# Seven of eight expert products as block products of a pair of token tiles, in a graph network with a mixture of experts

## The chip, the cores and the metric

One core of one Trainium2 chip runs the whole kernel in one launch. The metric is the device time in microseconds of that core: the median of several runs. A profiled execution gives a span, from its first to its last instruction, which is a little shorter.

## What is computed

`x` is 1250 x 512, there are 40,000 edges (`src`, `dst`), and 8 experts with a 512 x 512 weight each. All arithmetic is float32 in the reference.

```python
h = relu(layernorm(x) @ W1 + b1) @ W2 + b2          # 512 -> 256 -> 512
x = x + h + segment_sum(h[dst], src)                # row src collects h of dst
t = layernorm(x)
gate = softmax(t @ W_gate + b_gate); thr = 0.25 * sigmoid(t @ W_thr + b_thr)
w = relu(gate - thr); w = w / where(sum(w) == 0, 1, sum(w))
x = x + sum over e of w[:, e] * (t @ W_exp[e] + b_exp[e])
```

Every token goes through all 8 experts. The experts are most of the arithmetic.

## The kernel before, in words

The 1250 tokens are 10 tiles of 125 (`TILES`, `R`). Each engine has its own program, written out by hand, and the programs meet in semaphores.

**Head.** TensorE counts edges into an adjacency matrix: VectorE makes one-hot rows by comparison (L639), TensorE multiplies them (L908, float16, 250 columns, 50 windows), ScalarE copies the counts out (L431) and a DMA turns them into `a_t`. Between them stands the first linear layer (L856), and the aggregation (L870, float32) adds the tiles up in five PSUM banks. When the last window is counted, TensorE has 20 matmuls of aggregation left, then the degrees (L933), which need VectorE's sum of all `a_t` (L664, the last one waits for a DMA). VectorE copies the degrees (L685) and adds degree times `b2` to each of the ten tiles (L691). ScalarE copies the aggregate out (L480), and TensorE begins the second linear layer (L946, four tiles at once).

**Second normalization.** For each tile, VectorE adds the layer's output (L699), takes statistics (L705, L712), ScalarE the root (L484) and the normalized tile (L490), TensorE transposes it (L956, four blocks), ScalarE rounds the transposed tile to float16 as `xhi` (L495), VectorE takes the rest as `xlo` (L715), and TensorE multiplies both with the gate's weights (L965, L968). TensorE's order is: transposes of tile i, second layer of tile i + 4, gate of tile i - 1, and, from i = 6 on, a tile of expert 0. VectorE then works out the gate's weights for all tiles in a chain of small operations (L730 to L757), while TensorE goes on with expert 0 in seven banks.

**Experts.** A product in float32 quality is three float16 matmuls: high tokens with high weights, high with low, low with high (L990, L991, L992), summed in PSUM. A tile of an expert is 4 blocks of 128 inputs x 3 = 12 matmuls of 512 columns. Tokens are the stationary operand, loaded before each matmul. VectorE reads each finished tile once (L766: times the gate weight, added to `x_sb`) and adds the expert's bias (L771: `be_sb` in SBUF, times the gate weight). Four PSUM banks rotate. Experts 1 to 6 are a hardware loop of two experts a turn (`expert_loop`), 0 and 7 stand outside it. The weights of the next expert are fetched by SP into one of two stages (L300, 1 MB), rounded by ScalarE (L502: 2048 elements per partition, waiting for the last product that reads the buffer) and completed by VectorE in one operation in the middle of the pass before (L679). GpSimd makes constants in the first 8 us and does nothing after. In the last pass each tile leaves by two DMAs, 112 rows from SP (L331) and 13 from ScalarE's queue (L521), after its last addition.

## Time and profile before

| | us |
|---|---|
| three runs | 384.81, 385.31, 385.79; median 385.31 |
| profiled execution, span | 383.1 |
| profiled execution, its own run time | not recorded |
| TensorE busy | 367.2 (96%), 1892 matmuls |
| VectorE busy | 286.9 (75%) |
| ScalarE busy | 105.2 (27%) |
| GpSimd busy | 6.3 (2%) |
| DMA | 23.87 MB, mean 62 GB/s |

A matmul's record is longer than its turn: matmuls are pipelined, so the time that one costs is read from the distance between starts (or from the chain), not from its duration. The same holds in part for VectorE and ScalarE. The engines' names are PE (TensorE), PEld (its weight load), DVE (VectorE), ACT (ScalarE), POOL (GpSimd) and SP (the queue that starts DMAs); L12 is line 12 of the kernel. The number after the arrow at a line's end is idle time and what ended it.

### The profile page before, as it was taken

What the parts mean: (1) busy time and instruction counts of PE and PEld (TensorE: products, weight loads), DVE (VectorE), ACT (ScalarE), POOL (GpSimd) and SP (SyncE); (2) the same over time, 40 slices, a digit from 0 to 9 for tenths busy, and PEclk for the clock granted to TensorE, in tenths of its full rate; (3) what the DMA queues carried; (4) which work ended last, traced back from release to release, by engine and by line L of the source; (5) the groups of instructions that cost most, each with busy time, mean ns of one, the idle gap of its engine ahead of it and who ended that gap; (6) DMA issues with size and microseconds to landing.
All of it is one profiled execution on the core that took longest, in us unless ns stands there. A gap on an engine that the chain in (4) does not pass through costs nothing.

```text
span 383.1 us, 5937 instructions
## 1 busy us (share of the span) xinstructions
PE 367.2 (96%) x1892; PEld 239.3 (62%) x1892; DVE 286.9 (75%) x440; ACT 105.2 (27%) x189; POOL 6.3 (2%) x33
## 2 busy tenths in 40 slices
PE   2999999999999999999999999999999999999996
PEld 2777787656656563567656666666666666666663
DVE  6799987999999849972897756757657657576553
ACT  5843455556776204555010010010100100100000
POOL 6000000000000000000000000000000000000000
PEclk9999999999999999999999999999999999999999
DMA  8970011222222206300030300300302000000223
GB/s 222 202 245 19 16 39 44 77 69 78 76 72 85 84 15 158 133 34 2 1 111 0 109 2 1 109 0 1 108 0 96 14 0 0 0 0 0 81 84 104
DMA packets 16341, 23.87 MB, mean 62 GB/s; under 512 B 2169, under 2 KB 9216, under 8 KB 16193
## 3 DMA queue, kind: packets, MB, share of 16 engines
q1 hardware_dynamic: 15902, 23.05, 20.3%
q10 hardware_dynamic: 416, 0.53, 0.6%
q8 instruction: 12, 0.20, 0.2%
q14 instruction: 11, 0.09, 0.1%
HBM read 14.77 MB, written 2.56 MB: 45 GB/s over the span
## 4 chain that ended last, share of the span: by engine, by line
PE 80%; DVE 12%; issue 3%; DMA 2%; DVEq 2%; POOL 1%; ACT 0%; ACTq 0%; POOLq 0%
PE ps_g L990 17%; PE ps_g L991 17%; PE ps_g L992 17%; PE ps_g L870 10%; PE ps_w L908 9%; DVE split L639 3%; PE ps_g L856 3%; PE ps_g L946 2%; DMA x_sb<-in_x_dram 2%; DVE x_sb L691 2%; DVE stats L604 2%; DVE x_sb L766 1%; PE ps_w L900 1%; DVE x_sb L771 1%; PE ps_a L956 1%
## 5 line engine op out<-in xcount | busy, mean ns | idle before, releaser
L990 PE MATMUL ps_g<-we_hi,split 128*125 128x512 f16 x304 | 115.4, 380 | 0.7 <-DVE x_sb L766 0.7
L991 PE MATMUL ps_g<-we_lo,split 128*125 128x512 f16 x304 | 115.3, 379 | 0.0
L992 PE MATMUL ps_g<-we_hi,split 128*125 128x512 f16 x304 | 115.2, 379 | 0.0
L639 DVE TENSOR_TENSOR split<-places,keys 125x1536 f16<-125x1536 int16 (+2 forms) x125 | 91.1, 793 | 7.0 <-PE ps_w L908 4.2
L766 DVE SCALAR_TENSOR_TENSOR x_sb<-ps_g,weight_s,x_sb 125x512 f32<-125x512 f32 x76 | 56.9, 749 | 52.1 <-PE ps_g L992 52.1
L771 DVE SCALAR_TENSOR_TENSOR x_sb<-late,weight,x_sb 125x512 f32<-125x512 f32 x80 | 59.9, 750 | 9.5 <-DVE x_sb L766 5.5
L990 PEld LDWEIGHTS ps_g<-we_hi,split 128*125 128x125 f16 x304 | 41.5, 137 | 24.9 <-DVE x_sb L766 1.2
L992 PEld LDWEIGHTS ps_g<-we_hi,split 128*125 128x125 f16 x304 | 41.5, 137 | 24.1
L991 PEld LDWEIGHTS ps_g<-we_lo,split 128*125 128x125 f16 x304 | 41.5, 137 | 23.7
L908 PE MATMUL ps_w<-split 125*128 125x250 f16 x402 | 53.7, 270 | 2.5 <-DVE split L639 1.6
L908 PEld LDWEIGHTS ps_w<-split 125*128 125x128 f16 x402 | 36.9, 97 | 21.2 <-issue 9.4
L870 PE MATMUL ps_g<-late,r_sb 125*128 125x512 f32 (+3 forms) x120 | 49.1, 516 | 0.0
L502 ACT ACTIVATE we_hi<-stage 128x2048 f16<-128x2048 f32 x6 | 11.5, 1911 | 135.0 <-PE ps_g L992 120.9
L399 ACT ACTIVATE places<-iota_pos,win_base 125x512 int16<-125x512 int16 x50 | 35.7, 713 | 0.0
L431 ACT ACTIVATE counts<-ps_w 128x250 f32<-128x250 f32 x50 | 19.0, 379 | 32.0 <-PE ps_g L870 27.4
L870 PEld LDWEIGHTS ps_g<-late,r_sb 125*128 125x128 f32 x120 | 19.5, 191 | 7.8 <-issue 7.2
L856 PE MATMUL ps_g<-w_sb,x_t 128*125 128x256 f32 x80 | 19.7, 389 | 0.1
L679 DVE SCALAR_TENSOR_TENSOR we_lo<-stage,we_hi 128x2048 f16<-128x2048 f32 x8 | 18.3, 2285 | 0.0
L664 DVE TENSOR_TENSOR late<-late 125x1250 f32<-125x1250 f32 x9 | 13.1, 1454 | 4.9 <-DMA late<-counts 4.9
L856 PEld LDWEIGHTS ps_g<-w_sb,x_t 128*125 128x125 f32 x80 | 14.2, 187 | 2.1 <-issue 0.3
L946 PE MATMUL ps_g<-w_sb,early 128*125 128x512 f32 x32 | 14.8, 595 | 0.1
L900 PE MATMUL ps_w<-self_lo,self_pos 128*128 128x250 f16 x50 | 13.6, 273 | 0.7 <-ACT counts L431 0.7
(143 smaller groups left out, 220.2 us busy)
## 6 DMA issues: line engine op xcount, KB each, us to landing
stage<-in_L_ffn_W_exp_dram SPq DMA_DIRECT2D x8, 1024.0 KB, 5.2
late<-counts SPq DMA_DIRECT2D x50, 122.1 KB
x_sb<-in_x_dram SPq DMA_DIRECT2D x5, 448.0 KB, 11.3
out_dram<-x_sb SPq DMA_DIRECT2D x10, 224.0 KB
late<-in_L_ffn_b_exp_dram SPq DMA_DIRECT2D x1, 2000.0 KB
w_sb<-in_L_gnn_W_dram SPq DMA_DIRECT2D x2, 512.0 KB, 10.6
out_dram<-x_sb ACTq DMA_DIRECT2D x10, 26.0 KB
b_sb<-in_L_gnn_b_dram SPq DMA_DIRECT2D x1, 250.0 KB
```

What stands on the lines that cost most here:

```text
L399: nc.scalar.activation(places[w % WPT][:, :, 0:SEG], iota_pos[:, :, :], ACT.Identity, bias=win_base[:, w:w + 1], scale=1.0).then_inc(pos_r ...
L431: nc.scalar.activation(counts[q][:, :], ps_w[w % 2][:, 0:LO], ACT.Copy).then_inc(win_out, 1)
L639: nc.vector.tensor_tensor(hot[hot_at(w, p)][:, 0:n, :].rearrange("p c (k x j) -> p (c k) x j", k=SEGS, j=2), places[w % WPT][:, 0:n, :].re ...
L766: nc.vector.scalar_tensor_tensor(out=x_sb[:, i, :], in0=ps_first[FIRST_AT[i]] if first else ps_exp[(TILES * par + i) % RING], scalar=weigh ...
L771: nc.vector.scalar_tensor_tensor(out=x_sb[:, i, :], in0=be_sb[:, ds(e, 1), :], scalar=weight[:, i, ds(e, 1)], in1=x_sb[:, i, :], op0=ALU.m ...
L856: nc.tensor.matmul(r_bank[i % 2], x_t[i % XTS][:, k, :], w1_sb[:, k, :], start=(k == 0), stop=False)
L870: g = nc.tensor.matmul(ps_g[:, a:z], r_sb[:, i, c * 128:(c + 1) * 128], a_t[i % 3][:, a - c * SW:z - c * SW], start=opens, stop=False, ski ...
L908: mm = nc.tensor.matmul(bank[:, 0:LO], hot[hot_at(w, p)][:, c, 0:SEG], hot[hot_at(w, p)][:, c, SEG:SEG + LO], start=False, stop=False, ski ...
L946: y = nc.tensor.matmul(ps_y[i % YS], g_sb[:, c, tokens[i]], w2_sb[:, c, :], start=(c == 0), stop=(c == KC - 1))
L990: nc.tensor.matmul(bank, xhi[:, k, tokens[i]], hi_w, start=(k == 0), stop=False)
L991: nc.tensor.matmul(bank, xhi[:, k, tokens[i]], lo_w, start=False, stop=False)
L992: mm = nc.tensor.matmul(bank, xlo[:, k, tokens[i]], hi_w, start=False, stop=(k == KD - 1))
```

## The change

**Products.** Expert 0 stays as it was. For experts 1 to 7, two neighbouring tiles of tokens, left (A) and right (B), are taken as a 2 x 2 block matrix with two halves of 256 inputs each (a1, a2; b1, b2), the weight as 2 x 2 blocks of 256 x 256 (B11, B12, B21, B22). Strassen's algorithm in Winograd's form gives all four output blocks from seven products instead of eight. Weight sums: T1 = B12 - B11, T3 = B22 - B12, T2 = B22 - T1, T4 = B21 - T2. Token sums: S1 = b1 + b2, S3 = a1 - b1, S2 = S1 - a1, S4 = a2 - S2. Each product is 2 blocks of 128 inputs x 3 = 6 matmuls of 256 columns. Products share half banks: a bank is read (times the gate weight, into `x_sb`) after some products and goes on accumulating others, so intermediate states are added to several places. In a unit (a pair and an expert; there are 35) six reads result, five of 256 columns and one of 512. Two neighbouring units are interleaved. TensorE's stationary operand is 128 columns wide, the last three being the next tile's or zeros.

**Sums and halves.** GpSimd makes the four weight sums of every expert (128 x 512 float32 each) and the four token sums of every pair (2 x 125 each). ScalarE keeps a float32 copy `xt` of the transposed tile besides `xhi`, and rounds weights in three operations and token sums in one per pair. VectorE takes the low halves, weights in seven operations per expert of 512 elements, token sums in one per pair. For expert 1 this is in the head, between the last count and L685.

**Bias.** `be_sb` and the 80 operations of L771 go. The gate weights are split into high and low, transposed (10 transposes), and multiplied with three stacked copies of the bias (high, high, low): one matmul of 512 columns per tile, two in the first unit of experts 3 to 7, and one addition on VectorE each.

**Form.** The hardware loop over experts is gone; all units are written out. SP loads expert 2 before the bias, and waits for `wb_lo_done` for the others. Outputs leave after P3 (left tile) and P4 (right tile) of expert 7.

```diff
+            def block_sums(e):
+                w = stage[e % 2][:, :].rearrange("p (k f) -> p k f", k=KD)
+                b11, b12, b21, b22 = w[:, 0:2, 0:H], w[:, 0:2, H:D], w[:, 2:4, 0:H], w[:, 2:4, H:D]
+                pool.wait_ge(we_in[e % 2], 16 * (e // 2 + 1))
+                if e > 1:
+                    pool.wait_ge(wb_lo_done, BLOCKS * (e - 1))
+                nc.gpsimd.tensor_tensor(t_sum[:, T1 - T1, :, :], b12, b11, ALU.subtract).then_inc(t_added, 1)
...
+            pool.wait_ge(win_out, NW)
+            block_sums(1)
+            pool.wait_ge(r_done, TILES)
...
+            for j in range(PAIRS):
+                token_sums(j)
+            pool.wait_ge(y_done, TILES)
...
+            for e in range(2, EXP):
+                block_sums(e)
...
+            def high_blocks(e):
...
+                if e == 2:
+                    act.wait_ge(exp_done, TILES)
+                if e > 2:
+                    act.wait_ge(product_done, PRODUCT["P4", PAIRS * (e - 2) - 1])
+                nc.scalar.activation(hi[:, B11, :, :], w[:, 0:2, 0:H], ACT.Copy, scale=WSCALE).then_inc(wb_hi_done, 1)
...
+                act.wait_ge(t_added, 4 * e)
+                nc.scalar.activation(hi[:, T1:T4 + 1, :, :], t_sum[:, :, :, :], ACT.Copy, scale=WSCALE).then_inc(wb_hi_done, 1)
+            high_blocks(1)
             act.wait_ge(g_done, TILES)
...
+                nc.scalar.activation(xt[:, :, tokens[i]], turned_x, ACT.Copy).then_inc(xt_ready, 1)
+                nc.scalar.activation(xhi[:, :, tokens[i]], turned_x, ACT.Copy).then_inc(xhi_ready, 1)
...
+            for q in (B11, B21, B22):
+                low_block(1, q)
             column_sum(TILES - 1)
+            for q in (T1, T2, T3, T4):
+                low_block(1, q)
...
             dve.wait_ge(deg_done, 1)
...
+            for u in range(UNITS + 1):
...
+                lows = {1: (B11, B21), 2: (B22, T1), 3: (T2, T3), 4: (T4,)}.get(j, ()) if e < EXP - 1 else ()
+                if u < UNITS:
+                    add_product("P1", u, y, left, 0, H, 0)
...
+                if u >= 1:
+                    add_product("P7", u - 1, y_was, was_right, H, D, 0)
+                if lows:
+                    low_block(e + 1, lows[0])
...
+                if u >= 1:
+                    add_product("P3", u - 1, x_was, was_left, 0, D, 0)
+                if u < UNITS:
+                    add_product("P6", u, y, left, H, D, 0)
...
+                if u >= 1:
+                    add_product("P4", u - 1, y_was, was_right, 0, H, 0)
+                if lows[1:]:
+                    low_block(e + 1, lows[1])
+                if u < UNITS:
+                    add_product("P5", u, x, right, H, D, H)
...
+            def product(u, halves, q, out_cols, opens):
+                par = expert_of(u) % 2
+                for k, (hi_x, lo_x) in enumerate(halves):
+                    nc.tensor.matmul(out_cols, hi_x, wb_hi[par][:, q, k, :], start=(opens and k == 0), stop=False, skip_group_check=True)
+                    nc.tensor.matmul(out_cols, hi_x, wb_lo[par][:, q, k, :], start=False, stop=False, skip_group_check=True)
+                    mm = nc.tensor.matmul(out_cols, lo_x, wb_hi[par][:, q, k, :], start=False, stop=(k == 1), skip_group_check=True)
+                mm.then_inc(product_done, 1)
...
+            for u in range(UNITS + 1):
...
+                if bias:
+                    bias_tile(2 * (e - 3))
...
+                    pe.wait_ge(acc_step, Y_AFTER[u] if u < 4 else READ["P4", u - 4])
+                    product(u, (tile_of(left, 0), tile_of(left, 1)), B11, y, True)
...
+                    pe.wait_ge(acc_step, READ["P6", u - 1])
+                    product(u - 1, (sum_of(j_was, S3, 0), sum_of(j_was, S3, 1)), T3, y_was, False)
...
+                    pe.wait_ge(acc_step, X_AFTER[u] if u < 3 else READ["P3", u - 3])
+                    product(u, (tile_of(left, 2), tile_of(left, 3)), B21, x[:, 0:H], True)
...
+                    pe.wait_ge(acc_step, READ["P5", u - 1])
+                    product(u - 1, (sum_of(j_was, S4, 0), sum_of(j_was, S4, 1)), B22, x_was[:, H:D], False)
...
+                    pe.wait_ge(acc_step, READ["P1", u])
+                    product(u, (sum_of(j, S2, 0), sum_of(j, S2, 1)), T2, y, False)
...
+                    pe.wait_ge(acc_step, READ["P7", u - 1])
+                    product(u - 1, (tile_of(2 * j_was + 1, 2), tile_of(2 * j_was + 1, 3)), T4, y_was, False)
...
+                    product(u, (sum_of(j, S1, 0), sum_of(j, S1, 1)), T1, x[:, H:D], False)
```

In the order of the text the seven products of a unit are P1, P2, P6, P5 of the unit itself and P7, P3, P4 of the one before; TensorE's order in a step is P1, P7, P2, P3, P6, P4, P5.

## Rows read from the trace of the kernel before

**Rows 1.** Page, part 1: busy time of the engines.

```profile
PE 367.2 (96%) x1892; PEld 239.3 (62%) x1892; DVE 286.9 (75%) x440; ACT 105.2 (27%) x189; POOL 6.3 (2%) x33
```

**Rows 2.** Busy time by stretch; the columns are from:to, length, engines, clock, DMA.

```profile
131.00:144.00 13.00, 12.66 (x51) 7.35 (x49) 6.91 (x10) 0.81 (x4) 0.00 (x0) 1.00 0.12 33
...
181.60:197.95 16.35, 15.62 (x74) 9.62 (x72) 14.82 (x31) 1.35 (x4) 0.00 (x0) 1.00 0.06 10
...
197.95:379.46 181.51, 181.51 (x840) 114.62 (x840) 120.32 (x152) 10.78 (x6) 0.00 (x0) 1.00 0.12 41
...
379.46:383.10 3.64, 0.00 (x1) 0.00 (x0) 0.75 (x1) 0.00 (x0) 0.00 (x0) 1.00 0.24 74
```

**Rows 3.** Groups by line in the stretch of experts 1 to 7.

```profile
L766 DVE SCALAR_TENSOR_TENSOR x_sb<-ps_g,weight_s,x_sb 125x512 f32<-125x512 f32 x72 | 53.9, 749 | 52.1 <-PE ps_g L992 52.1
```

**Rows 4.** Timeline at the start of expert 1 and at the end; start, duration, instruction.

```profile
196.84 0.38 PE L992 MATMUL ps_w<-we_hi,split 128*125 128x512 f16 x1
...
197.95 0.43 PE L990 MATMUL ps_g<-we_hi,split 128*125 128x512 f16 x1 [0.73 <-DVE x_sb L766]
...
379.08 0.38 PE L992 MATMUL ps_g<-we_hi,split 128*125 128x512 f16 x1
...
379.57 0.75 DVE L766 SCALAR_TENSOR_TENSOR x_sb<-ps_g,weight_s,x_sb 125x512 f32<-125x512 f32 x1 [1.18 <-PE ps_g L992]
```

**Rows 5.** Timeline, from the last count to the second linear layer.

```profile
131.12 7.86 PE L870 MATMUL ps_g<-late,r_sb 125*128 125x512 f32 x20
...
131.30 2.29 DVE L679 SCALAR_TENSOR_TENSOR we_lo<-stage,we_hi 128x2048 f16<-128x2048 f32 x1
...
132.25 0.38 ACT L431 ACTIVATE counts<-ps_w 128x250 f32<-128x250 f32 x1 [1.13 <-PE ps_g L870]
...
137.01 1.46 DVE L664 TENSOR_TENSOR late<-late 125x1250 f32<-125x1250 f32 x1 [3.43 <-DMA late<-counts]
...
141.31 6.71 DVE L691 SCALAR_TENSOR_TENSOR x_sb<-b_sb,deg,x_sb 125x512 f32<-125x512 f32 x10
...
143.69 2.38 ACT L480 ACTIVATE early<-ps_g 128x250 f32<-128x250 f32 x3 [11.07 <-PE ps_g L870]
```

**Rows 6.** Chain that ended last, one burst of L908; start, us, what.

```profile
58.38 1.07 PE ps_w L908 x10
```

**Rows 7.** Page, part 5: the edge counting's matmul and its weight load.

```profile
L908 PE MATMUL ps_w<-split 125*128 125x250 f16 x402 | 53.7, 270 | 2.5 <-DVE split L639 1.6
...
L908 PEld LDWEIGHTS ps_w<-split 125*128 125x128 f16 x402 | 36.9, 97 | 21.2 <-issue 9.4
```

**Rows 8.** Timeline, one tile of the second normalization.

```profile
159.24 0.63 PE L956 MATMUL ps_w<-ident,xn 125*128 125x125 f32 x4
...
159.90 0.59 ACT L495 ACTIVATE split<-ps_w 128x500 f16<-128x500 f32 x1 [1.14 <-PE ps_w L956]
...
160.39 0.80 ACT L490 ACTIVATE xn<-x_sb,shift,rstd 125x512 f32<-125x512 f32 x1
...
160.53 0.68 DVE L715 TENSOR_TENSOR split<-ps_w,split 128x500 f16<-128x500 f32 x1 [0.39 <-ACT split L495]
...
161.42 0.35 PE L965 MATMUL ps_g<-wg,split 128*125 128x18 f16 x4
...
161.86 0.63 PE L956 MATMUL ps_a<-ident,xn 125*128 125x125 f32 x4
...
162.32 1.88 PE L946 MATMUL ps_g<-w_sb,early 128*125 128x512 f32 x4
```

**Rows 9.** Timeline of VectorE: the gate's first operation and expert 0's first read.

```profile
181.67 0.25 DVE L730 SCALAR_TENSOR_TENSOR lg_b<-ps_g,bg_sb 125x90 f32<-125x90 f32 x1 [2.17 <-PE ps_g L968]
...
186.17 0.75 DVE L766 SCALAR_TENSOR_TENSOR x_sb<-ps_g,weight_s,x_sb 125x512 f32<-125x512 f32 x1
```

**Rows 10.** Groups by line and shape: ScalarE's rounding, GpSimd's largest operation.

```profile
L502 ACT ACTIVATE we_hi<-stage 128x2048 f16<-128x2048 f32 x6 | 11.5, 1911 | 135.0 <-PE ps_g L992 120.9 <-PE ps_w L992 14.1
...
L381 POOL TENSOR_SCALAR_AFFINE_SELECT self_lo<-self_lo 25x475 f16<-25x475 f16 x1 | 0.8, 779 | 0.0
```

More of the change, by code:

```diff
@@ L101, in gnn_moe @@
         win_base = sb("win_base", [EP, NW])
-        places = [sb(f"places{q}", [EP, PART, HOT], I16) for q in range(WPT)]
+        places_all = sb("places", [128, WPT * PART * HOT], I16)
+        places = [places_all[0:EP, q * PART * HOT:(q + 1) * PART * HOT].rearrange("p (c h) -> p c h", c=PART) for q in range(WPT)]
         base_row = sb("base_row", [ROWS, NW])
@@ L473, in _ @@
                     act.wait_ge(we_in[0], 16)
-                    nc.scalar.activation(we_hi[0][:, :], stage[0][:, :], ACT.Copy, scale=WSCALE).then_inc(we_hi_done, 1)
+                    nc.scalar.activation(we_hi, stage[0][:, :], ACT.Copy, scale=WSCALE).then_inc(we_hi_done, 1)
                 if w == 32:
@@ new lines, in _ @@
+            for i in range(TILES + 2):
+                if i >= 2:
+                    turn(i - 2)
+                if 1 <= i <= TILES:
+                    norm(i - 1)
+                if i < TILES:
+                    deviation(i)
+                if i in SUMS_AT:
+                    high_sums(SUMS_AT[i])
+            act.wait_ge(logits_ready, 1)
+            nc.scalar.activation(ex[:, :, :], lg_c[:, :, :], ACT.Exp).then_inc(exps_ready, 1)
+            nc.scalar.activation(te[:, :], lg_a[:, :, EXP], ACT.Exp, scale=-1.0).then_inc(exps_ready, 1)
@@ new lines, in _ @@
+            for j in range(len(SUMS_AT), PAIRS):
+                high_sums(j)
+            act.wait_ge(weight_ready, 1)
+            nc.scalar.activation(w_hi[:, :, :], weight[:, :, :], ACT.Copy).then_inc(w_hi_done, 1)
+            act.wait_ge(w_hi_done, 1)
+            nc.scalar.activation(w_3[:, :, 0:2 * EXP].rearrange("p t (r e) -> p t r e", r=2),
+                                 w_hi[:, :, :].unsqueeze(2).broadcast_to([R, TILES, 2, EXP]), ACT.Copy).then_inc(w_3_ready, 1)
+            high_blocks(2)
@@ new lines, in _, with tile_of, sum_of @@
+            gate(TILES - 1)
+            for i in range(RING, TILES):
+                first_expert(i)
+            def tile_of(i, k):
+                at = k * N + i * R
+                return split[:, at:at + 128], split[:, KD * N + at:KD * N + at + 128]
+            def sum_of(j, c, k):
+                return s_hi[:, j, c, k, :], s_lo[:, j, c, k, :]
+            def product(u, halves, q, out_cols, opens):
[5 more added lines that the diff above has]
+                mm.then_inc(product_done, 1)
@@ new lines, in turn_weights, with bias_tile @@
+            def turn_weights(g):
+                a, z = W_GROUPS[g]
+                if g == 0:
+                    pe.wait_ge(w_3_ready, 2)
+                    pe.wait_ge(acc_step, TILES)
+                else:
+                    pe.wait_ge(w_t_ready, g)
+                for i in range(a, z):
+                    t = nc.tensor.transpose(ps_spare[0:KB, (i - a) * R:(i - a + 1) * R], w_3[:, i, :], ident[0:R, 0:R])
+                t.then_inc(w_turned, 1)
+            def bias_tile(i):
+                if i == 0:
+                    pe.wait_ge(w_t_ready, len(W_GROUPS))
+                    pe.wait_ge(be_ready, 1)
+                else:
+                    pe.wait_ge(bias_added, i)
+                nc.tensor.matmul(ps_spare[0:R, :], w_t[:, tokens[i]], be_3[:, :], start=True, stop=True).then_inc(bias_done, 1)
```

355 lines of the change are left out of this document (225 added, 130 removed).

## The prediction

> **What bounds it now.** I first read the share of the engines on the page [rows 1], then the busy time by stretch [rows 2]: TensorE is busy 96% of the span, at the full granted clock in every stretch, and the stretch from 197.95 to 379.46 us, which holds experts 1 to 7, has 840 matmuls in 181.51 us without a gap. That is 0.2161 us for one of 512 columns. VectorE is busy 120.32 us there and ScalarE 10.78. The waits of the same stretch [rows 3] say who follows whom: VectorE spends 52.1 us waiting for the last matmul of a tile. So TensorE's columns set this part, and a column saved is time saved as long as VectorE keeps up. The rest of the time goes to 3.64 us after the last matmul, of which 0.75 is one VectorE operation and nearly all else the output's transfer [rows 2, 4], and to a head of 198 us in which two places hang on VectorE: the ten additions of L691, before which nothing of the second normalization can start, and the start of expert 1, which waited for the reading of expert 0's tile 8 [rows 4, 5].
>
> **Experts 1 to 7 on TensorE.** Before, a pair of tiles takes 24 matmuls of 512 columns. After, it takes seven products of six matmuls of 256 columns: 42, or 7/8 of the columns. What decides is whether 256 columns really cost half. The nearest row is the edge counting of L908: ten matmuls of 250 columns with a weight load each take 1.07 us in the chain, 0.107 each [rows 6]. Between 0.107 for 250 and 0.216 for 512 columns, 256 columns come to 0.1095 us. The load (97 ns for 128 columns [rows 7]) stays below that, and the gate's eight tiny matmuls with their eight loads follow each other in 0.44 us, 0.055 a pair [rows 8], so neither issue nor loading is the bound at 0.1095. 35 pairs x 42 x 0.1095 = 161.0 us against 181.5: **-20.5 us**. The ends: 0.1067 (3.9 less) and 0.137, if the load at the duration that it has for 125 columns could not hide (40 more).
>
> The Trainium skill ("TensorE: Matmul & The Clock Gate", Back-to-back issue gap) says that in a stream of load and matmul pairs a short matmul costs clearly more than its columns: about 81 ns at 128 columns where columns alone would give 56, and 131 ns at 512. By a surcharge of 25 ns, a pair here would cost about 134 ns, the products 197 us, and the change would lose 16 us where I count a gain. The trace speaks against both figures: 512 columns take 216 ns, 250 take 107.
>
> **Bias on TensorE.** Ten matmuls of 512 columns, 10 x 0.216 = 2.2 us, and ten transposes at a quarter of the 0.45 us that four take between L956 and L946, 1.1 us [rows 8]. The second matmul of a bias pair writes the bank that VectorE must first have read: VectorE has to finish P7 (0.5) and the addition (0.68) before it, and TensorE has 1.3 us of products meanwhile, so about 0.1 us is lost five times. **+3.8 us**, from 3.3 to 5.
>
> **VectorE beside it.** The 70 additions of L771 in these passes go. A read of 256 columns isn't in the trace: 90 columns took 0.25 and 512 take 0.75 [rows 4, 9], by the line between them 0.44; I take 0.49. A pair costs 5 x 0.49 + 0.75 = 3.2 us, the four-part work on the next expert's low halves 7 x 0.75 = 5.3 us per expert (a block of 512 columns at L766's price), at most two blocks = 1.5 us in a pair: 4.7 us in the busiest pair against TensorE's 4.60, as durations. But followers start before durations end (L691: ten in 6.71, 0.66 each where one lasts 0.75) [rows 5], which brings that pair to about 4.0, and a mean pair to 3.8. So no stall in general; each product that reuses a half-filled bank has two or three other products, 1.31 to 1.97 us, in front of it, against 0.28 (from the end of the columns to VectorE's start [rows 4]) + 0.49 + 0.1 for the read. Only pair 0, which has no neighbour, loses 0.2. Nothing for the loads: a 1 MB stage is asked for a pass earlier than it is used. ScalarE's three copies per expert (3584 elements, about 3.6 us by 1.91 for 2048 [rows 10]) and GpSimd's four sums (about 5 us) have 23 us per pass; if that cover were gone they would add their own 8 us to each pass, which needs them to be several times dearer.
>
> **Start of expert 1.** Before, the last matmul of expert 0 started at 196.84 and ended its columns at 197.06, and the next came at 197.95 [rows 4], since VectorE was behind with 2.29 us of low weights (the length of the one in [rows 5]) and the bias additions. Both are gone from there (two blocks of token sums at about 1.2 each come in). -0.9 + 0.2 for pair 0: **-0.7 us**.
>
> **Head: GpSimd's block sums.** This is the cost I am least sure of. After the last count (132.25 + 0.38 = 132.6 [rows 5]) GpSimd makes four sums of 128x512 for expert 1, three of them in a chain with the first; ScalarE then rounds them (1.9 us for 2048 elements), VectorE takes four differences, and only behind these stand L685 and L691, which set the end. GpSimd with two operands isn't in the trace: its one-operand operation on 475 columns took 0.78 us [rows 10]. From below 512 columns cost 0.84, from above twice that, 1.7; I take 1.2, nearer the one-operand row. 132.7 + 4 x 1.2 = 137.5, + 0.2 for the waits, + 1.9 = 139.6, + 4 x 0.61 + 0.14 = 142.2, + a reduction and the copy 0.3 = 142.5; L691 began at 141.31: +1.2 us. With 1.7 it is +3.2. VectorE's own three first blocks (133.5 to 135.5) and L664 (137.01, 1.46 us) read two SBUF operands while GpSimd reads its own. Nothing in the trace shows the two engines together. If they exclude each other, each waits for the other's operation, about 3 x 0.7 for GpSimd, +3.3, and L664 may start 1 us late, which TensorE (busy with L870 until 138.98) would feel after 0.4. I take **+2.5 us**, ends 1 and 6. ScalarE is due at 143.69 for L480 and is done with expert 1's halves by 139.6 to 142: covered, by 2 us.
>
> The Trainium skill ("SBUF — State Buffer", Who interferes with whom) states just such a lock, for VectorE operations with two SBUF inputs against a GpSimd that reads; by it the head would cost about 4 to 5 us in place of 2.5. A product read has one operand in PSUM, so by that page the passes would be untouched.
>
> **Second normalization.** ScalarE copies each turned tile twice and VectorE's L715 comes one copy later. The loop that could matter: transposes at 159.24, ScalarE at 159.90, two copies (0.49 apart) until the norm at 160.88 instead of 160.39, end 161.69, next transposes due at 161.86 [rows 8]. Under 0.2 us is left, so the period of 2.62 just holds. VectorE idles 0.39 a tile and its L715 moves by 0.49; the shift that ScalarE needs then still comes 0.4 early. From the seventh tile the period is 2.59 + 0.46 + 0.44 = 3.5 us and takes the high and low sums (about 1.0 and 1.2). GpSimd's token sums, 250 columns each, may hold up L715 or the gate's chain, which has 2.5 us: its first read ends at 186.92 [rows 9], and TensorE needs that bank after three more tiles of 2.59 behind the gate's 181.67, at 189.4. **+0.5 us**, from 0 to 4.
>
> **Tail.** In the last, unpaired step P3 waits for P5's read behind one product only (0.87 - 0.66 = 0.2), and P4 for P7's likewise. The final read is 0.26 shorter, the last two tiles' transfers lie closer together (0.3). **+0.5 us**, up to 1.5.
>
> **Sum.** -20.5 + 3.8 - 0.7 + 2.5 + 0.5 + 0.5 = -13.9, on the profiled span of 383.1: 369.2 us. The median of the runs, 385.31, stands 2.2 above this span, and the profiled execution's own time is not shown, so I add 2.2: **371.4 us**. Its own range, from the ends that are plausible together, is 368 to 376.
>
> **Rivals.**
> 1. *GpSimd and VectorE hold each other up* through head, normalization and gate: head +6, normalization +3, gate chain past its 2.5 us by 1, two waits a pass (1 us): +8, so about 379. For it: L679 and L664 lie exactly where the sums will be; against it: most of these waits have cover. Chance 0.17.
> 2. *The pair of load and matmul costs slightly more than its columns* in a stream of 1470, 0.115 in place of 0.1095: +8, 379. For it: the row of L908 has only ten in a row; against it: those ten keep 0.107, and 512 columns keep 0.216 over 840. Chance 0.06.
> 3. *VectorE becomes the bound: slower.* Its place is the pair with six reads and two blocks, its price the half-width read: if a read is mostly fixed cost, six take 0.75 each, 35 x 6 x 0.75 = 157.5, + 42 low blocks x 0.75 = 31.5, + 6.8 for bias = 195.8 us against TensorE's 164.8, so 369.2 + 31 + 2.2 = 402 us. It decides as soon as reads and blocks don't overlap and a half read costs over about 0.6. Against it: 90 columns in 0.25. Chance 0.04.
> 4. *The saving doesn't come* (sums or low parts late at every expert, TensorE waiting at each pass's first product): 7 passes x 2 us, 385. GpSimd would have to be four times slower than its row. Chance 0.02.
>
> My forecast has 0.71. A measurement here can tell about 0.3%, 1.2 us. Faster by more: 0.93; within: 0.03; slower: 0.04. To hold eight in ten the range takes in part of the first two rivals: 367.5 to 378.
>
> **What would show it.** In the changed profile: the products' matmuls at 0.109 us start to start and each pass near 23 us (23.4 with bias); L691's counterpart starting at 142.5 to 145; the first product at about 200, right behind expert 0; VectorE about 75 to 85% busy in the passes, with waits for TensorE; GpSimd's 512-column sum at 1.2 us; the last matmul some 14 us earlier than 379.08. I am wrong if TensorE shows waits for VectorE in every pair, if the spacing is above 0.112, or if a GpSimd sum lasts over 2 us.

## The result and the profile after

The changed kernel takes 374.75 us (median of four runs, 374.42 to 375.82) against 385.55 (384.81 to 385.92) for the kernel before: ratio 0.9726, 95% interval 0.9709 to 0.9744. The forecast of 371.4 us was 3.4 us too low; the measured time lies inside its range, 367.5 to 378. The profiled execution took 375.82 us, the slowest of the four, with a span of 374.0 us against 383.1; the forecast span was 369.2.

The page of the changed kernel, its parts 1 and 2 (busy time; 40 slices of 9.35 us each):

```profile
PE 354.1 (95%) x2542; PEld 270.7 (72%) x2542; DVE 320.9 (86%) x561; ACT 128.0 (34%) x224; POOL 61.9 (17%) x87
...
POOL 6000000000000070063680005040050410500000
PEclk9999999999999997999999999999999999999999
```

GpSimd, idle before but for the very start, now works in slice 15, in slices 18 to 21 and in bursts behind them. Right behind slice 15 the clock's row has a 7, where the row of the kernel before is all 9. Now the busy time by stretch, cut at the same events as [rows 2]: expert 0's low weights (now L805) start, first transposes of the normalization, first operation of the gate (L876), first product, last product's columns, end. The columns are from:to, length, engines, clock, DMA share, GB/s.

```profile
130.98:156.26 25.28, 22.98 (x68) 11.32 (x66) 23.61 (x33) 7.54 (x11) 6.83 (x8) 0.86 0.20 59
156.26:186.70 30.44, 30.30 (x194) 19.91 (x193) 24.06 (x53) 22.90 (x41) 15.19 (x18) 1.00 0.11 38
186.70:204.63 17.93, 15.60 (x72) 9.57 (x71) 16.69 (x29) 2.88 (x6) 8.29 (x9) 1.00 0.00 0
204.63:369.98 165.35, 165.24 (x1491) 145.21 (x1489) 137.77 (x264) 22.30 (x22) 25.29 (x20) 1.00 0.12 39
369.98:374.00 4.02, 0.16 (x2) 0.00 (x0) 0.69 (x2) 0.00 (x0) 0.00 (x0) 0.88 0.40 127
```

The kernel before had its first transposes at 151.84, which bounds its head in the table:

```profile
151.84 0.65 PE L956 MATMUL ps_a<-ident,xn 125*128 125x125 f32 x4 [0.24 <-ACT xn L490]
```

| us, profiled executions | before | after | difference | forecast |
|---|---|---|---|---|
| up to the low weights | 131.30 | 130.98 | -0.3 | 0 |
| head, to the first transposes | 20.54 | 25.28 | +4.7 | +2.5 |
| second normalization | 29.83 | 30.44 | +0.6 | +0.5 |
| gate and expert 0, to the first product | 16.28 | 17.93 | +1.65 | -0.7 |
| experts 1 to 7 | 181.35 | 165.35 | -16.0 | -16.7 |
| tail | 3.8 | 4.02 | +0.2 | +0.5 |
| span | 383.1 | 374.0 | -9.1 | -13.9 |

So the saving in the passes came nearly whole. The 4.8 us missing from the forecast are 0.7 in the passes and 4.6 in two stages ahead of them, less 0.5 elsewhere.

**The passes.** Groups by line and shape, busy time and mean ns of one, then idle time ahead:

```profile
L1196 PE MATMUL ps_g<-wb_hi,places 128*128 128x256 f16 x212 | 57.8, 273 | 0.1
...
L920 DVE SCALAR_TENSOR_TENSOR x_sb<-ps_g,weight_s,x_sb 125x256 f32<-125x256 f32 x107 | 50.2, 480 | 9.8 <-PE ps_g L1198 8.6
...
L1196 PEld LDWEIGHTS ps_g<-wb_hi,places 128*128 128x128 f16 x212 | 20.8, 98 | 3.2 <-DVE x_sb L920 0.6 <-issue 0.3
```

TensorE is busy 165.24 of 165.35 us, VectorE 137.77 (83%), and VectorE's idle time ends with TensorE (L1198), not the other way. The mean matmul of 273 ns is no spacing, since pipelined matmuls overlap; the spacing is the stretch divided by its work.

**The head.** Timeline of the changed kernel (start, duration, instruction; in brackets the idle time ahead and what ended it); it answers to [rows 5]:

```profile
132.72 1.67 POOL L443 TENSOR_TENSOR t_sum<-stage 128x512 f32<-128x512 f32 x1
...
133.18 5.11 DVE L813 SCALAR_TENSOR_TENSOR wb_lo<-stage,wb_hi 128x512 f16<-128x512 f32 x3
...
137.82 1.59 POOL L448 TENSOR_TENSOR t_sum<-stage,t_sum 128x512 f32<-128x512 f32 x1
...
138.21 2.52 DVE L791 TENSOR_TENSOR late<-late 125x1250 f32<-125x1250 f32 x1
...
139.44 1.91 ACT L586 ACTIVATE wb_hi<-t_sum 128x2048 f16<-128x2048 f32 x1 [5.38 <-POOL t_sum L448]
...
140.78 2.34 PE L1109 MATMUL ps_a<-ones,late 125*125 125x1 f32 x20 [1.20 <-DVE late L791]
142.99 3.94 PE L1046 MATMUL ps_g<-late,r_sb 125*128 125x226 f32 x8
144.05 6.71 DVE L830 SCALAR_TENSOR_TENSOR x_sb<-b_sb,deg,x_sb 125x512 f32<-125x512 f32 x10
```

Three of VectorE's blocks last 5.11 us, from GpSimd's first sum to its last. L791, the sum of `late` that took 1.46 us at L664, takes 2.52, and the degrees (L1109) find TensorE idle for 1.20 us. L830 starts at 144.05, 2.74 later than L691 did. What it waited for is the chain behind GpSimd's sums: the last one ends at 139.41, ScalarE's rounding (L586) at 141.35, VectorE's last block at 143.88; the degrees were there at 143.1. Then eight matmuls of L1046 take 3.94 us. Busy time by stretch says why:

```profile
143.00:147.00 4.00, 3.93 (x10) 1.69 (x9) 3.96 (x9) 0.03 (x1) 0.00 (x0) 0.67 0.00 0
147.00:151.00 4.00, 3.51 (x4) 1.48 (x5) 3.77 (x6) 2.35 (x3) 0.00 (x0) 0.50 0.00 0
```

The last column but two is the granted clock: 0.50, the 1.2 GHz level, from about 144.2 to 151.2 us.

**The gate.** Timeline of the same kernel behind expert 0's eighth tile:

```profile
188.39 1.77 DVE L885 TENSOR_SCALAR te<-te 125x10 f32<-125x10 f32 x1 [0.45 <-ACT te L627]
188.54 1.63 DVE L886 TENSOR_REDUCE ex_sum<-ex 125x10 f32<-125x80 f32 x1
189.00 1.14 POOL L475 MEMSET early<- 128x1250 f16 x1
190.10 1.26 POOL L443 TENSOR_TENSOR t_sum<-stage 128x512 f32<-128x512 f32 x1
...
191.50 1.19 DVE L894 SCALAR_TENSOR_TENSOR adapted<-te,soft 125x80 f32<-125x80 f32 x1
...
192.72 1.15 DVE L896 TENSOR_SCALAR picked<-adapted 125x80 f32<-125x80 f32 x1
...
196.01 2.07 DVE L909 SCALAR_TENSOR_TENSOR x_sb<-ps_g,weight_s,x_sb 125x512 f32<-125x512 f32 x3
196.81 0.43 PE L1162 MATMUL ps_g<-wb_hi,split 128*125 128x512 f16 x1 [2.33 <-DVE x_sb L909]
```

An operation on ten elements a partition (L885) lasts 1.77 us and ends with GpSimd's memset; the next ones end with GpSimd's sums for expert 2. The gate's chain, from L876 at 186.70 to L909 at 196.01, takes 9.3 us where it took 4.5 [rows 9], and TensorE stands idle for 2.33 us.

My theory was thus: GpSimd and VectorE hold each other up in the head and behind the gate, and nowhere else does it cost; the rival was that late results, a DMA or the clock by itself make these delays.

### The profile page after: what moved, and what is told of

Its sections match the earlier page's. It is cut to its first block, busy times and chain, and to the rows that moved or that the text cites. A ratio compares the mean times of both kernels' runs of the same rounds, so it can differ in the third digit from the quotient of the medians.

```text
span 374.0 us, 7335 instructions
## 1 busy us (share of the span) xinstructions
PE 354.1 (95%) x2542; PEld 270.7 (72%) x2542; DVE 320.9 (86%) x561; ACT 128.0 (34%) x224; POOL 61.9 (17%) x87
## 3 DMA queue, kind: packets, MB, share of 16 engines
q1 hardware_dynamic: 15820, 21.05, 19.1%
## 4 chain that ended last, share of the span: by engine, by line
PE 78%; DVE 11%; issue 4%; DMA 2%; DVEq 2%; ACT 1%; POOL 1%; ACTq 0%; POOLq 0%
PE ps_g L1196 10%; PE ps_g L1198 10%; PE ps_g L1197 10%; PE ps_g L1046 9%; PE ps_w L1084 8%; DVE split L766 4%; PE ps_g L1122 3%; PE ps_g L1032 3%; PE ps_a L1196 2%; DMA x_sb<-in_x_dram 2%; PE ps_a L1198 2%; PE ps_a L1197 2%; PE ps_w L1196 2%; PE ps_w L1198 2%; PE ps_w L1197 2%
## 5 line engine op out<-in xcount | busy, mean ns | idle before, releaser
L920 DVE SCALAR_TENSOR_TENSOR x_sb<-ps_g,weight_s,x_sb 125x256 f32<-125x256 f32 (+1 forms) x142 | 75.1, 546 | 19.6 <-PE ps_g L1198 18.4
L1196 PE MATMUL ps_g<-wb_hi,places 128*128 128x256 f16 x212 | 57.8, 273 | 0.1
L1197 PE MATMUL ps_g<-wb_lo,places 128*128 128x256 f16 x212 | 57.8, 273 | 0.0
L1198 PE MATMUL ps_g<-wb_hi,r_sb 128*128 128x256 f16 x212 | 57.8, 273 | 0.0
L1046 PE MATMUL ps_g<-late,r_sb 125*128 125x512 f32 (+3 forms) x120 | 50.5, 527 | 0.5 <-DMA late<-counts 0.5
L1196 PE MATMUL ps_g<-wb_hi,split 128*128 128x256 f16 x142 | 38.7, 273 | 0.0
L1197 PE MATMUL ps_g<-wb_lo,split 128*128 128x256 f16 x142 | 38.7, 273 | 0.0
L1198 PE MATMUL ps_g<-wb_hi,split 128*128 128x256 f16 x142 | 38.7, 273 | 0.0
L1046 PEld LDWEIGHTS ps_g<-late,r_sb 125*128 125x128 f32 x120 | 19.8, 193 | 8.8 <-issue 8.1
L1196 PEld LDWEIGHTS ps_g<-wb_hi,places 128*128 128x128 f16 x212 | 20.8, 98 | 3.2 <-DVE x_sb L920 0.6
L1197 PEld LDWEIGHTS ps_g<-wb_lo,places 128*128 128x128 f16 x212 | 20.7, 98 | 2.6
L1198 PEld LDWEIGHTS ps_g<-wb_hi,r_sb 128*128 128x128 f16 x212 | 20.7, 98 | 2.4
L920 DVE SCALAR_TENSOR_TENSOR x_sb<-ps_a,weight_s,x_sb 125x256 f32<-125x256 f32 x36 | 17.3, 481 | 4.3 <-PE ps_a L1198 3.7
```

What stands on the lines that cost most here:

```text
L920: nc.vector.scalar_tensor_tensor(out=x_sb[:, i, a:z], in0=bank[0:R, at:at + z - a], scalar=weight_s[:, expert_of(u), i:i + 1], in1=x_sb[:, ...
L1046: g = nc.tensor.matmul(ps_g[:, a:z], r_sb[:, i, c * 128:(c + 1) * 128], a_t[i % 3][:, a - c * SW:z - c * SW], start=opens, stop=False, ski ...
L1196: nc.tensor.matmul(out_cols, hi_x, wb_hi[par][:, q, k, :], start=(opens and k == 0), stop=False, skip_group_check=True)
L1197: nc.tensor.matmul(out_cols, hi_x, wb_lo[par][:, q, k, :], start=False, stop=False, skip_group_check=True)
L1198: mm = nc.tensor.matmul(out_cols, lo_x, wb_hi[par][:, q, k, :], start=False, stop=(k == 1), skip_group_check=True)
```

## The experiments

**One: the block sums of expert 1 ahead of the counts.** They move from behind the last count to behind window 24 of the 50, so that VectorE has the time behind the last count to itself.

```diff
+            pool.wait_ge(win_out, 24)
+            block_sums(1)
             pool.wait_ge(win_out, NW)
             nc.gpsimd.memset(split[...], 0.0).then_inc(s_pads, 1)
-            block_sums(1)
```

> Expert 1's four GpSimd block sums run during the edge counting (after window 24) in place of behind the last window; nothing else moves. Theory A (GpSimd and VectorE exclude each other on operations that read two SBUF operands, and the wait that this gives TensorE at the degrees lets its clock fall): the three low blocks of L813 take about 2 us in place of 5.1, L791's counterpart takes 1.46 in place of 2.52 and starts at about 137.0, TensorE's gap before the degrees goes, the granted clock stays 1.00 from 143 to 151 us, the additions of L830's counterpart start at about 141.5, the first transposes at about 152 in place of 156.3; whole time 374.75 - 4.4 = about 370.3 us. Theory B (only the length of the chain sums, rounding, low parts in front of the additions, TensorE's clock falls for another reason): the additions start 2.7 us earlier, but the clock still falls, so 372. Theory C (it was TensorE's own work): no change, 374.7. If the lock also holds in the counting, the comparisons that the sums meet get longer there by up to 5 us in total, which TensorE, the bound of those windows, hides.

Measured: 373.78 us (372.79 to 375.13), ratio 0.9695 [0.9663, 0.9726], span 371.0. The head's stretch and its timeline:

```profile
132.07:153.12 21.05, 20.11 (x69) 10.23 (x66) 18.61 (x31) 7.34 (x11) 0.26 (x4) 1.00 0.24 71
```

```profile
138.28 1.46 DVE L792 TENSOR_TENSOR late<-late 125x1250 f32<-125x1250 f32 x1 [1.76 <-DMA late<-counts]
140.09 2.24 PE L1110 MATMUL ps_a<-ones,late 125*125 125x1 f32 x20
142.58 6.71 DVE L831 SCALAR_TENSOR_TENSOR x_sb<-b_sb,deg,x_sb 125x512 f32<-125x512 f32 x10
```

The head fell from 25.28 to 21.05, the sum of `late` is back at 1.46, TensorE has no gap and the clock stays full. But the median gained only about 1.2 us. The timeline of GpSimd and VectorE at the sums' new place shows where part of the rest went:

```profile
90.41 18.21 POOL L443 TENSOR_TENSOR t_sum<-stage 128x512 f32<-128x512 f32 x1 [82.38 <-ACT counts L527]
...
107.86 2.08 DVE L792 TENSOR_TENSOR late<-late 125x1250 f32<-125x1250 f32 x1 [0.36 <-issue]
108.58 2.48 POOL L444 TENSOR_TENSOR t_sum<-stage 128x512 f32<-128x512 f32 x1
```

The first sum hung for 18.21 us (18.13 to 18.21 in the four traces with this edit) while VectorE issued one two-operand instruction after the other (comparisons and two sums of `late`), and came through only after VectorE's one pause there, at 107.5; the others then held VectorE up. From 108 to 115 us TensorE is busy 5.68 us here and 7.00 in the changed kernel. The low weights start at 132.07 to 133.02 us in the four traces with this edit and at 129.83 to 131.83 in the eight without. The lock was moved, not removed. But in experiment ten, which has no sums in the counting, the low weights start at 132.63 as well, so the later start needn't be the lock's alone. The two profiled executions aren't alike either: the change's was the slowest of its four (span 374.0 us, the others 372.6 to 373.0), this one's the fastest of its six. The intervals of the two ratios overlap, so the times by themselves don't show a gain.

**Two: the gate's chain kept free.** GpSimd's sums over the tokens of pairs 3 and 4, its memsets and all that follows wait until the gate is done; ScalarE's rounding of these pairs goes behind the gate too.

```diff
-            for j in range(PAIRS):
+            for j in range(3):
+                token_sums(j)
+            pool.wait_ge(weight_ready, 1)
+            for j in range(3, PAIRS):
                 token_sums(j)
...
```

> GpSimd is quiet while VectorE works out the gate: the token sums of pairs 3 and 4, the two memsets and expert 2's block sums wait for the finished gate weights (ScalarE's rounding of those two pairs moves behind the weights too). Theory A (exclusion): the chain from the first gate operation to the first read of expert 0 is 4.5 us as in the kernel before, in place of 9.3, TensorE's gap of 2.3 us at 194.4 goes, whole time 374.75 - 2.3 = about 372.4 us. Theory B (the chain is long because ScalarE's two exponentials came late, behind its roundings): those operations stay where they are in the order, so the chain stays at about 9 us and the time at 374.7. If both hold in part, 373.5.

Measured: 371.87 us (371.0 to 374.32), ratio 0.9659 [0.9621, 0.9697], span 369.2. The stretch from the gate to the first product:

```profile
184.46:199.85 15.39, 15.39 (x72) 9.65 (x71) 12.33 (x28) 3.10 (x6) 11.06 (x13) 1.00 0.00 0
```

17.93 became 15.39, TensorE is busy all of it, and the median fell by what the stretch gave, 0.0067 x 385.6 = 2.6 us. The gate's chain is as short as before the change again, and the clock fell in this head also (24.02 us).

**Three: both edits.**

> Both edits together. Theory A: the two losses lie one behind the other on the same path, so they add: 374.75 - 4.4 - 2.3 = about 368.0 us, span about 367.3, first block product at about 198 us. Rival: the second is covered by the first (an earlier head runs into another limit, such as the low token sums before the gate), 370.

Measured: 371.84 us (370.22 to 373.7), ratio 0.9646 [0.9608, 0.9685], span 368.4. Busy time by stretch, for head and gate:

```profile
132.11:153.09 20.98, 20.06 (x68) 10.17 (x65) 18.59 (x31) 7.28 (x11) 0.26 (x4) 1.00 0.24 71
...
183.61:199.00 15.39, 15.39 (x72) 9.65 (x71) 12.32 (x28) 3.10 (x6) 11.06 (x13) 1.00 0.00 0
```

Against experiment two the head is 3.0 us shorter but starts 2.1 later (132.11 against 129.99), and the medians are the same. Six runs of this kernel spread over 3.5 us, five of them at a mean clock of 1.00; so the clock isn't all that varies.

**Four and five: does the gap ahead of the degrees bring the clock down?** Six idle matmuls in it, then twelve.

```diff
+            for _ in range(6):
+                nc.tensor.matmul(ps_a[:, 0:2 * LO - WIN], self_pos[:, 0:SEG], self_lo[:, :], start=True, stop=True)
             pe.wait_ge(a_summed, TILES - 1)
```

> The changed kernel with six matmuls of 475 float16 columns that are multiplied for nothing, in TensorE's gap of 1.2 us before the degrees; the waits stay. It separates the clock from the wait. If the gap is what lets the granted clock fall, the clock stays at 1.00 between 143 and 151 us, aggregation's last eight matmuls take 2.7 in place of 3.9 us and the first four of the second layer 1.9 in place of 3.75, and the time comes down by 2 to 3 us (up to 1 less if the matmuls outlast the gap): about 372.5. If the twenty one-column matmuls of the degrees are what lets it fall, the clock falls all the same and the time stays at 374.7 or rises by 0.3.

> As the run with six idle matmuls before the degrees, but twelve (2.4 us of 475 columns each), so that TensorE has no gap at all between the aggregation's four matmuls and the degrees. With six, a gap of 0.43 us was left and the clock fell to half at 143.0. Theory A (any gap there together with the one-column matmuls of the degrees lets it fall): the clock stays at 1.00, the last eight matmuls of the aggregation take 2.7 us in place of 4.3, from the low weights of expert 0 to the first transposes it is 24.2 - 1.6 + up to 0.8 (the idle matmuls outlast the gap) = about 23.4 us. Theory B (the earlier gap at 137, where TensorE waits for the transfer of the last counts, is what counts): the clock falls again and the stretch stays at 24.2 to 25.

Measured: 375.25 us, 0.9726 [0.9692, 0.976], for six; 376.72 us, 0.9754 [0.9714, 0.9794], for twelve. The timeline with six:

```profile
140.99 2.43 PE L1111 MATMUL ps_a<-ones,late 125*125 125x1 f32 x20 [0.43 <-DVE late L791]
143.28 4.33 PE L1046 MATMUL ps_g<-late,r_sb 125*128 125x226 f32 x8
```

and with twelve:

```profile
141.88 2.24 PE L1111 MATMUL ps_a<-ones,late 125*125 125x1 f32 x20
143.99 2.73 PE L1046 MATMUL ps_g<-late,r_sb 125*128 125x226 f32 x8
```

With 0.43 us of gap the clock fell all the same, with none it stayed, in this one profile. No time was won: the twelve outlast the gap (the degrees start at 141.88 where they started at 140.78), and in that profile the clock fell behind the gate instead (19.63 us for 17.93).

**Six: a stationary of 125 columns**, whose load takes longer. It tests the prediction's upper end for the spacing.

```diff
-                    nc.tensor.matmul(out_cols, hi_x, wb_hi[par][:, q, k, :], ...)
+                    nc.tensor.matmul(out_cols[0:R, :], hi_x[:, 0:R], wb_hi[par][:, q, k, :], ...)
```

> The changed kernel with stationary operands of 125 columns in place of 128 in all block products (the outputs' three spare rows aren't written). It tests the upper end of the price that the prediction set for one matmul of 256 columns. Theory A (the weight load hides behind 256 columns whatever its length): spacing stays at 0.109 us, whole time 374.7. Theory B (the load of 125 columns lasts 137 ns, more than 109, and cannot hide): spacing 0.137, 1470 x 0.028 = 41 us more, 416 us. In between: spacing 0.115 to 0.12, 383 to 390.

Measured: 376.19 us (374.99 to 378.57), 0.9766 [0.9731, 0.9801]. The load's group and the passes' stretch:

```profile
L1196 PEld LDWEIGHTS ps_g<-wb_hi,places 128*125 128x125 f16 x212 | 29.0, 137 | 0.7 <-DVE x_sb L920 0.5 <-issue 0.2
```

```profile
205.41:370.84 165.43, 165.33 (x1491) 162.44 (x1489) 137.77 (x264) 22.31 (x22) 25.28 (x20) 1.00 0.12 39
```

The load grew from 98 to 137 ns, longer than the 109 that a matmul has, and the passes by 0.08 us, less than 0.1 ns for each of the 1470 products' matmuls. So 137 ns of load is no bound on the spacing, and the columns are. The median is 1.4 us above the change's. By this profile that lies outside the passes (the head took 25.85 us), and the intervals overlap.

**Seven: no bias matmuls**, nor the ten additions of their results on VectorE, which hang on the same flag. The result then lacks the experts' bias.

```diff
-                bias = j == 0 and 3 <= e < EXP
+                bias = False
...
```

> The changed kernel without the ten bias matmuls and the ten additions of their results (the experts' bias is left out of the result; the transposes of the gate weights stay). By the prediction's sum they cost 10 x 0.216 + 5 x 0.1 = 2.7 us of TensorE's time: 372.0. By the trace of the changed kernel, which shows TensorE's loads waiting 1.4 us for the additions, 2.2 + 1.4 = 3.6: 371.1. If the bias were hidden in other waits: 374.5.

Measured: 372.93 us (372.34 to 374.57), 0.9675 [0.9647, 0.9703].

```profile
206.09:368.23 162.14, 162.04 (x1481) 144.33 (x1479) 131.29 (x254) 22.31 (x22) 25.29 (x20) 1.00 0.13 40
```

The passes fell by 3.2 us. Ten matmuls are 2.16 of it; the other 1.05 must be waits: the trace of the changed kernel has 1.4 us of them in its list, where the weight loads of the second bias matmuls wait for VectorE (sum in us, times, longest):

```profile
PEld ps_w L1220 <- DVE x_sb L914: 1.4, 5, 0.3
```

What is left, 162.14, is the forecast's 161.0 for 1470 products and 1.1 for ten transposes: 0.1095 us a matmul, as taken.

**Eight: the block sums of experts 2 to 7 on VectorE**, four operations in pair 0 of the pass before, none on GpSimd.

```diff
-            for e in range(2, EXP):
-                block_sums(e)
...
+                if sums:
...
+                    nc.vector.tensor_tensor(t_sum[:, T1 - T1, :, :], b12, b11, ALU.subtract).then_inc(t_added, 1)
...
```

> The changed kernel with the block sums of experts 2 to 7 on VectorE (four operations of 512 columns in the first pair of each pass) and only expert 1's on GpSimd. It asks what GpSimd is worth in the passes and how far VectorE is from being the bound. By the prediction's sum VectorE has 23.4 - 19 us free per pass and the first pair has no low blocks: 5 x 0.49 + 0.75 + 4 x 0.7 = 6.0 us of work in a pair of 4.6 us, less overlap about 5.2, so TensorE waits about 0.6 to 1.5 us in each of six passes, from which the GpSimd sums' collisions at the gate (about 0 to 2 us) come off: 376 to 382. Rival (VectorE has room for all of it, so GpSimd only does harm): the time falls to 372.5, as GpSimd no longer has expert 2's sums in the gate's chain.

Measured: 375.17 us (373.5 to 376.13), 0.9721 [0.969, 0.9752]. Gate and passes:

```profile
186.75:202.14 15.39, 15.39 (x72) 9.65 (x71) 13.45 (x29) 2.88 (x6) 3.38 (x5) 1.00 0.00 0
202.14:369.88 167.74, 165.85 (x1491) 144.78 (x1489) 148.02 (x288) 22.97 (x22) 0.00 (x0) 1.00 0.12 39
```

A trade without profit: 2.5 us won at the gate, 2.4 lost in the passes. It says two things. At the gate it is the block sums of expert 2 that push the chain past its cover; token sums and memsets alone (still there) leave no gap. And in the passes GpSimd is the right place: its 25 us cost TensorE nothing.

**Nine: does the fetch of expert 2 touch the clock or the head?** Both edits, with the fetch behind the last sum of `late`.

```diff
             sp.wait_ge(we_lo_done, 1)
+            sp.wait_ge(a_summed, TILES - 1)
             load_expert(2)
```

> Both repairs, and SP's fetch of expert 2's weights (1 MB) waits until all counts have arrived and are summed, in place of starting at 133.4, beside the last counts' transfers. Theory (the fetch slows these transfers): the last addition of counts starts about 4.8 us after ScalarE's last copy of counts, as in the kernel before, in place of 5.0 to 5.4, and the stretch from the low weights to the first transposes goes from 21.0 to 20.5 us; the time falls by 0.5 against the run with both repairs, ratio to the kernel before about 0.963. Rival (no effect of the fetch): 21.0 us stay.

Measured: 371.87 us (371.42 to 372.45), 0.964 [0.9614, 0.9665].

```profile
140.47 2.24 PE L1112 MATMUL ps_a<-ones,late 125*125 125x1 f32 x20
142.57 4.42 PE L1049 MATMUL ps_g<-late,r_sb 125*128 125x226 f32 x8
```

```profile
133.02:154.77 21.75, 21.14 (x65) 10.81 (x64) 19.46 (x33) 7.31 (x10) 0.25 (x4) 0.92 0.21 68
...
143.00:146.50 3.50, 3.50 (x8) 1.59 (x6) 3.50 (x6) 0.00 (x0) 0.00 (x0) 0.52 0.43 167
```

No time from the fetch. The last sum of `late` starts 4.44 us after ScalarE's last copy of counts here and 4.92 in experiment three, so the counts may have landed half a microsecond earlier; but the head took 21.75 us for the expected 20.5, and the median stayed. And here the clock fell right behind the degrees although TensorE had no gap ahead of them.

**Ten: the sums alone, in the kernel before.** Four GpSimd subtractions of 128x512 into a spare tile behind the last count.

```diff
...
+            pool.wait_ge(we_in[1], 16)
+            pool.wait_ge(win_out, NW)
+            for n in range(4):
+                nc.gpsimd.tensor_tensor(t_spare[:, n, :, :], w[:, 0:2, D // 2:D], w[:, 0:2, 0:D // 2], ALU.subtract).then_inc(spare_added, 1)
```

> The kernel before the change with one thing added: four GpSimd subtractions of 128x512 float32 on expert 1's stage, right behind the last count, into a spare tile that nobody uses. It asks whether GpSimd's presence alone brings the lock and the clock. Theory A (exclusion): L679 (low weights, two SBUF operands) and GpSimd's first operation wait for each other, and L664 at 137.0 waits for the operation that GpSimd has running, up to 1.3 us; TensorE gets a gap of about 0.1 to 0.9 us before the degrees, and if that is enough for the clock to fall, the stretch to the first transposes grows by 2 to 4 us: 387 to 389 in place of 385.4; if the clock holds, by 0 to 1: 385.5 to 386.3. Rival (no exclusion, what was slow in the head was the kind of low block): L664 keeps its start and its 1.46 us, GpSimd's operations last 1.26 each, time unchanged.

Measured: 385.87 us (384.76 to 388.2, 12 runs) beside 385.95 (384.44 to 388.0, 17 runs), 1.000 [0.9977, 1.0024].

```profile
133.55 7.38 POOL L389 TENSOR_TENSOR t_spare<-stage 128x512 f32<-128x512 f32 x4 [125.57 <-ACT counts L438]
137.73 2.08 DVE L672 TENSOR_TENSOR late<-late 125x1250 f32<-125x1250 f32 x1 [2.81 <-DMA late<-counts]
139.86 2.34 PE L941 MATMUL ps_a<-ones,late 125*125 125x1 f32 x20 [0.15 <-DVE late L672]
142.06 4.42 PE L878 MATMUL ps_g<-late,r_sb 125*128 125x226 f32 x8
```

The lock is there (four sums in 7.38 us, `late` in 2.08), but TensorE waits 0.15 us for it and the time doesn't change. In the changed kernel it costs because VectorE also has its own three blocks in front of `late`, and because rounding and low blocks wait for the sums. Eight matmuls in 4.42 us: the clock fell in this profile too. It isn't the change that brought this: of the 48 runs of the unmodified kernel before beside the experiments, 22 have a mean clock of 0.990 to 0.996 and a median of 386.50 us, the other 26 at least 0.998 and 385.18.

**Eleven and twelve: wide degrees.** The twenty matmuls of one column become 128 columns wide, on the kernel with both edits and on the changed kernel.

```diff
-                dg = nc.tensor.matmul(ps_a[0:R, i:i + 1], a_sum[...], ones[0:R, 0:1], ...)
+                dg = nc.tensor.matmul(ps_a[0:R, i:i + 128], a_sum[...], ones[0:R, 0:128], ...)
```

> Both repairs, and the ten degree products have 128 equal columns in place of one (each overwrites all columns but the first of the one before, so the degrees stay where they were). Up to here the clock fell behind these products in most profiles: with a gap before them, and once without. Theory A (it is the stretch of one-column products, in which the array does next to nothing, that lets the granted clock fall; it then depends on the run whether it does): the twenty records take 2.2 to 2.4 us as before, the clock stays at 1.00 until the second normalization in the profile, and the timed runs close up at the fast end of the run with both repairs: 370.2 to 371.2, median 370.7, ratio about 0.961. Theory B (the gap, or the fetch, lets it fall): no change in clock or spread, median 371.8. If wider products take longer than narrow ones (0.14 us in place of 0.11), up to 0.6 us are lost.

> The changed kernel itself with the 128-column degree products and nothing else; the gap of about 1.2 us before them, the lock and the late additions stay. Theory A (one-column products let the clock fall): the clock stays at 1.00 from 143 us on, the aggregation's last eight matmuls take 2.7 us, and the time falls by 1 to 2 us to about 373 to 373.7. Theory B (gap): the clock falls as before, 374.7.

Measured: 371.73 us (370.74 to 372.74), 0.965 [0.9621, 0.968], with both edits; 375.14 us (373.15 to 376.08), 0.9733 [0.9703, 0.9762], without. The profile of the latter:

```profile
139.64 2.45 PE L1109 MATMUL ps_a<-ones,late 125*125 125x128 f32 x20 [0.91 <-DVE late L791]
141.93 2.65 PE L1046 MATMUL ps_g<-late,r_sb 125*128 125x226 f32 x8
```

Full clock in both profiles, even behind 0.91 us of gap, and no gain in either median. Three of the five runs of the latter had a mean clock of 0.993 to 0.994, as the changed kernel has (0.990 to 0.995). That narrow matmuls bring the clock down isn't shown.

**The best version** is the changed kernel with both edits, with or without the fetch's wait: 0.9646 and 0.964 of the time before, about 3 us below the change. Experiment two alone (0.9659) can't be told from them; the second edit is the one whose gain is clear of noise.

## Why the prediction came out as it did

**Experts 1 to 7: right.** 256 columns cost 0.1095 us, taken between two rows at 0.107 and 0.216. The longer spacing that the Trainium skill states for a short matmul in a stream with weight loads ("TensorE: Matmul & The Clock Gate", Back-to-back issue gap) is not in this stream: 0.1095 us a pair, where the prediction's estimate from that page was 134 ns. The second rival (0.115) fell with that spacing, the upper end of 0.137 with experiment six. The lower end, 0.1067, would be 4.1 us less, not 3.9. **Bias: mis-sized by 0.5 us**: experiment seven leaves 0.2 us for the wait at the bank each time, not 0.1. **VectorE: right**, a read of 256 columns took 0.48 us (taken 0.49), and it is busy 83% of the passes; the third rival fell.

**Head: the delay right, what follows it missing.** From the start of the low weights to the ten additions it is 13.07 us where it was 10.01 (141.31 less 131.30 [rows 5]), +3.1 for the 2.5 taken, with the lock seen in the trace and undone by experiment one. A sum without VectorE beside it takes 1.26 us (taken 1.2), with it 1.6 to 1.7; the four took 6.69 us, from 132.72 to 139.41, where 4.8 were taken: 1.9 more, beside the 1.2 that the chain was to cost without a lock. Behind the additions the stretch took 12.21 us where the kernel before and experiment one took 10.5: 1.7 us of lower clock. In experiments two and four, where the clock fell for half as long, it took 10.95 and 11.13. No step had the clock. The Trainium skill ("SBUF — State Buffer", Who interferes with whom) states this lock, and the trace agrees. That the prediction's estimate from it, 4 to 5 us, lies nearer the whole +4.7 is luck: the lock's share is the 3.1, the rest is the clock.

**Start of expert 1: the step that failed.** I took -0.7 and it came to +1.65. What goes (low weights, bias additions) I counted rightly: without the collision the stretch is 15.39 us, 0.9 less than the 16.28 of before. But I named only the token sums as a danger for the gate's chain, which "has 2.5 us". Behind these GpSimd starts the memsets and the block sums of expert 2 at once, 1.7 and 5 us, and they fall on the chain: 4.5 us became 9.3, past the cover by 2.33. Experiments two and eight show it, by different edits with the same 15.39. What I hadn't made is a list of everything that GpSimd has queued behind the moved work.

**Normalization and tail** came within 0.3 us. The first rival's mechanism, at the chance of 0.17, is what happened at two of its three places, with no wait in the passes: +4.6 of its +8, of which 1.7 are the clock. **Span to median:** I added 2.2 us, and the profiled execution stood 1.8 above its span; the median of after lies 1.1 below that execution, so that the forecast's distance is 4.8 us by spans and 3.4 by medians; that the median is the nearer one is luck. Of the signs named, the first product came at 204.63, not at about 200, and the last matmul at 369.87, 9.2 us earlier than before and not 14; the others came as written, but for a GpSimd sum beside VectorE (1.6 to 1.7 us for 1.2).

**Open:** what brings the clock down behind the degrees. It fell in the profiles of the change and of experiments two, four, six to ten, and not in those of the kernel before, one, three, five, eleven and twelve. In these profiles a gap of 1.20 us or more goes with a fall of 6.8 us (the change, and six, seven and eight, where it begins among the degrees), a smaller one or none with a fall of 3.4 (two, four, nine, ten) or with no fall; but neither filling the gap nor widening the matmuls changed a median. The mean clock is at least 0.998 in 15 of the 22 runs with experiment one's edit and in 7 of the 45 without it: a link to that edit, not a cause, as experiment nine has the edit and such a clock in one run of five. That the first edit is worth less than its stretch is shown; how much of the remainder is the lock further ahead is argued from the traces, as no run has the sums at a third place.

## What to carry to other kernels

When work moves to an idle engine, write down all that this engine then does in a row, and lay it against every short chain of the engine that it shares memory with, down to operations of ten elements: here two memsets and four sums, 6.7 us together, made a chain of 4.5 us 4.8 longer. Whether a wait is covered isn't seen from the mean share of busy time. Look where the chain stands alone, here between the gate and the first weighted result. And in a stream like this one, with a weight load for each matmul of 256 columns, count columns.

## What the runs showed of the hardware

- A two-operand GpSimd sum hung while VectorE issued two-operand instructions without a pause: 18.21 us for a sum that takes 1.26, ended behind VectorE's first pause (experiment one). The other way VectorE lost less per instruction: 1.46 us became 2.08 to 2.52.
- Some VectorE operations of 10 to 80 elements a partition grew from 0.17 to 0.24 us to 0.8 to 1.8 beside GpSimd, one of them beside a token sum and two memsets (the change).
- A weight load of 137 ns hid behind matmuls spaced at 0.109 us over 1470 pairs (experiment six).
- The granted clock fell to 0.52 of full, mean of 3.5 us, behind twenty one-column matmuls in 2.24 us with no idle time ahead (experiment nine), and in the same place of the same order of work it stayed full (experiment three).
